# Where the TensorE operands of an attention and mixture-of-experts kernel begin in the on-chip memory

## The reference

```python
# layer 1, on layernorm(x); 4 heads of 128
Q, K, V = xh @ Wh, kh @ Wh, vh @ Wh            # the same Wh for all three
masked = (Q @ K.T / sqrt(128)) * decay_mask
A = maximum(abs(masked.sum(batch)), 1.0)       # summed over the 4 batches
O = A @ V;  Y = normalize(O) * gamma + beta
x = x + (relu(xn @ wg_w) * Y) @ wo_w
# layer 2, on layernorm(x): mixture of experts, 2048 tokens
scores = softmax(xt @ Wg.T)                    # 16 experts in 4 groups
# the 2 best groups, then the 4 best experts of them for each token
h = silu(xt @ W1[e].T) * (xt @ W3[e].T)        # 512 -> 352
y = sum over the 4 experts of weight * (h @ W2[e].T)
z = silu(xt @ Ws1.T) * (xt @ Ws3.T) @ Ws2.T    # shared, 2 x 352 wide
x = x + y + z
```

## The kernel before

| tensor | role on TensorE | before | after | rest before | rest after |
|---|---|---|---|---|---|
| `whi`, `wlo` | moving, experts | 88800, 123616 | 88832, 123648 | 32, 32 | 0, 0 |
| `xhi`, `xlo`, p = 0 | stationary, up | 166624, 170720 | 166656, 170816 | 32, 32 | 0, 0 |
| `xhi`, `xlo`, p = 1 | stationary, up | 168672, 172768 | 168736, 172896 | 32, 32 | 32, 32 |
| `hhi`, `hlo` | stationary, down, even | 178528, 180064 | 178688, 180224 | 32, 32 | 0, 0 |
| `hhi_odd`, `hlo_odd` | stationary, down, odd | 202144, 203680 | 202336, 203872 | 32, 32 | 32, 32 |
| `wg_hi`, `wg_lo` | moving, gate | 88800, 96992 | 88832, 97024 | 32, 32 | 0, 0 |
| `xn_hi`, `xn_lo` | stationary, gate | 158432, 162528 | 158464, 162560 | 32, 32 | 0, 0 |
| `q_hi`, `q_lo` | moving, scores | 52960, 61152 | 52992, 61184 | 32, 32 | 0, 0 |
| `ctx_hi`, `ctx_lo` | stationary, scores | 207776, 215968 | 207808, 216000 | 32, 32 | 0, 0 |
| `wo_hi`, `wo_lo` | moving, projection | 141568, 149760 | 141632, 149824 | 0, 0 | 0, 0 |
| `xT`, `xT_lo` | stationary, projection | 215968, 220064 | 216000, 220096 | 32, 32 | 0, 0 |

## Time and profile before

### The profile page before, as it was taken

How to read it: one execution, slowest core, us unless ns; L and a number is a source line. 1 busy time by engine, 2 the same in 40 slices (tenths; PEclk the granted TensorE clock), 3 DMA queues, 4 the chain that set the end, 5 groups by cost and what they waited for, 6 DMA issues and landing times.

```text
span 919.3 us, 19365 instructions
## 1 busy us (share of the span) xinstructions
PE 899.9 (98%) x4962; PEld 806.1 (88%) x4963; DVE 557.9 (61%) x1105; ACT 332.0 (36%) x708; POOL 494.3 (54%) x346
## 2 busy tenths in 40 slices
PE   8999998899989999999999999999999999999998
PEld 5777887687889999999999999999999999989997
DVE  6656767888896644544444444444444444459997
ACT  4556554354324322333333333333333333332221
POOL 1127777874167764434646664456666643136772
PEclk9999999999999999999999999999999999999999
DMA  6829996665569956878778776788777755588984
GB/s 214 264 106 385 388 403 251 230 189 172 184 227 297 308 206 207 243 205 247 245 235 252 248 246 203 237 244 258 248 251 249 248 170 158 163 231 241 275 254 144
DMA packets 180649, 218.97 MB, mean 238 GB/s; under 512 B 56576, under 2 KB 124160, under 8 KB 180224
## 3 DMA queue, kind: packets, MB, share of 16 engines
q1 hardware_dynamic: 118080, 123.49, 41.9%
q0 software_dynamic: 20816, 79.44, 26.1%
q10 hardware_dynamic: 41712, 15.54, 6.3%
HBM read 127.38 MB, written 91.03 MB: 238 GB/s over the span
## 4 chain that ended last, share of the span: by engine, by line
PE 80%; DVE 9%; issue 4%; ACT 3%; DMA 3%; ACTq 0%; DVEq 0%; POOL 0%; SPq 0%; POOLq 0%
PE ps L1170 15%; PE ps L1171 15%; PE ps L1172 15%; PE ps L1222 8%; PE ps L1224 8%; PE ps L1223 8%; PE ps L1019 2%; PE ps L1035 2%; PE ps L966 1%; DVE st L1469 1%; DVE res L1467 1%; PE ps L1055 1%; PE ps L1057 1%; PE ps L1056 1%; DVE st L1284 1%
## 5 line engine op out<-in xcount | busy, mean ns | idle before, releaser
L1170 PE MATMUL ps<-whi,xhi 128*128 (+1 forms) x888 | 288.8, 325 | 1.2 <-issue 0.6
L1172 PE MATMUL ps<-whi,xlo 128*128 (+1 forms) x888 | 286.7, 323 | 0.0
L1171 PE MATMUL ps<-wlo,xhi 128*128 (+1 forms) x888 | 286.7, 323 | 0.0
L1544 DVE TENSOR_TENSOR hrow<-ps,sg 128x352 f32<-128x352 f32 x95 | 49.7, 523 | 214.1 <-ACT sg L838 214.1
L1170 PEld LDWEIGHTS ps<-whi,xhi 128*128 128x128 f32 x888 | 167.7, 189 | 6.1 <-issue 1.3
L1171 PEld LDWEIGHTS ps<-wlo,xhi 128*128 128x128 f32 x888 | 167.7, 189 | 3.9
L1172 PEld LDWEIGHTS ps<-whi,xlo 128*128 128x128 f32 x888 | 167.3, 188 | 0.0
L838 ACT ACTIVATE sg<-ps 128x352 f32<-128x352 f32 x111 | 51.5, 464 | 268.1 <-PE ps L1172 268.0
L845 ACT ACTIVATE xhi<-ps 128x512 fp32r<-128x512 f32 x112 | 66.9, 597 | 145.8 <-DVE ps L1505 145.7
L566 POOL TENSOR_TENSOR wlo<-raw,whi 128x2816 fp32r<-128x2816 f32 x16 | 100.7, 6291 | 2.4 <-POOL whi L564 0.9
L658 POOL DMA_INDIRECT raw<-yslot_d,sloti x64 | 67.7, 1058 | 57.7 <-DMA yslot_d<-ysb 22.6
(11 more groups left out here) (201 smaller groups left out, 1583.4 us busy)
## 6 DMA issues: line engine op xcount, KB each, us to landing
raw<-wexp_in POOLq DMA_DIRECT2D x18, 2176.0 KB, 11.1
xslot_d<-zero SPq DMA_DIRECT2D x10, 2048.0 KB, 21.6
xg<-xslot_d SPq DMA_DIRECT2D x320, 64.0 KB, 2.8
yslot_d<-ysb SPq DMA_DIRECT2D x80, 256.0 KB, 2.4
h_d<-hrow ACTq DMA_DIRECT2D x79, 192.0 KB, 3.0
hblk<-h_d SPq DMA_DIRECT2D x79, 192.0 KB, 2.5
xg<-xn_d SPq DMA_DIRECT2D x128, 64.0 KB, 3.7
xq<-x_in SPq DMA_DIRECT2D x16, 256.0 KB, 3.3
```

The source lines that it names most:

```text
L1170: pe.matmul(ps[:, bank, 0:INTER], xh, wh, start=(k == 0), stop=False)
L1171: pe.matmul(ps[:, bank, 0:INTER], xh, wl, start=False, stop=False)
L1172: mm = pe.matmul(ps[:, bank, 0:INTER], xl, wh, start=False, stop=(k == KT - 1))
```

## The change

Three pads are added (`line_pad`, `odd_pad`, `row_pad`, each 32 bytes in a partition), `heads_keep` grows by 48 bytes, and each half of `xhi` and `xlo` grows by 32 bytes, so that the second half starts 32 bytes past a multiple of 64; the two instructions that write whole halves take the first 512 columns. No instruction is added, removed or moved on any engine: without the line numbers the lists of instructions of the two programs are the same. What differs is addresses, those of the table above and of all tensors named behind `line_pad`: input tiles, sums and buffers of the other engines too. Line numbers behind the pads grow by 1 to 3.

```diff
         cbf = keep("cbf", [P, 2, P], BF16)
+        keep("line_pad", [P, Q // 4], F32)
         res = keep("res", [P, NT * D], F32)
...
-            late.enter_context(nc.sbuf_tensor("heads_keep", [P, KT * D + B * S + 2 * HCOL + AT_COL + HD + H * S + B + 2 * D], F32))
+            late.enter_context(nc.sbuf_tensor("heads_keep", [P, KT * D + B * S + 2 * HCOL + AT_COL + HD + H * S + B + 2 * D + 12], F32))
...
-        xhi = sb3("xhi", [P, 2, KT * P], F32R)
-        xlo = sb3("xlo", [P, 2, KT * P], F32R)
+        xhi = sb3("xhi", [P, 2, KT * P + Q // 4], F32R)
+        xlo = sb3("xlo", [P, 2, KT * P + Q // 4], F32R)
...
         scat = sb3("scat", [P, XR, D], F32)
+        sb3("odd_pad", [P, Q // 4], F32)
         hhi.append(sb3("hhi_odd", [P, IC * P], F32R))
         hlo.append(sb3("hlo_odd", [P, IC * P], F32R))
+        sb3("row_pad", [P, Q // 4], F32)
         hrow = sb3("hrow", [P, 2, IC * P], F32)
...
-                    act.activation(xhi[:, p, :], ps[:, p, :], ACT.Copy).then_inc(x_hi, 1)
+                    act.activation(xhi[:, p, 0:KT * P], ps[:, p, :], ACT.Copy).then_inc(x_hi, 1)
...
-                    dve.tensor_tensor(xlo[:, p, :], ps[:, p, :], xhi[:, p, :].bitcast(F32), ALU.subtract).then_inc(x_lo, 1)
+                    dve.tensor_tensor(xlo[:, p, 0:KT * P], ps[:, p, :], xhi[:, p, 0:KT * P].bitcast(F32), ALU.subtract).then_inc(x_lo, 1)
```

## The result

The kernel after takes 924.94 us (median of 20 runs), the kernel before 921.25 us (20 runs). The ratio is 1.003, with a 95% interval from 1.0019 to 1.0041: slower by about 0.3%, 1.8 to 3.8 us. The forecast was 921.5 us, no change, with a range of 907 to 929 us. So the time lies in the range, which is wide, and just about at the bound of 0.3% that the prediction drew between "the same" and "slower"; the interval excludes no change at all.

A forecast was written before the change was run, and what follows sets the result against it. TensorE's matmul pace was taken to bound the kernel's expert tiles. Terms 2.0 + 1.3 - 2.2 - 0.7 = +0.4 us on the 919.3 us span gave 919.7; with 1.8 for the median, 921.5 us, range 907 to 929.

The forecast's parts named there:

- the order of the two down sets: Expert tiles, sign in the timeline: even down set goes to 2.06 us and odd one to 2.10, reversing their order.
- That only TensorE's pace counts: Expert tiles: only the matmuls' own pace counts; the other engines were given 0, in the front part too.
- Odd down, +2.0 us from the projection's row: Odd expert tiles, down sets: operands half a line apart cost 4.1 ns a matmul, as in the projection, +2.0 us.
- Odd up, +1.3 us from 1 ns each: Odd expert tiles, up sets: 1 ns a matmul, taken between 0 and 4.1 ns, +1.3 us.
- Even down, -2.2 us: Even expert tiles, down sets: leaving their slow place gains 4.4 ns a matmul, -2.2 us, other end 0.
- three of four places: At 512 columns, places with operands in the same or a near place said to give 229 to 230 ns.
- Even up, 0: Even expert tiles, up sets: no change, staying at 3.83 us a set.
- Moving operands at the start of a line, 0 between -27 us and a little above: Even tiles and front part: one 64-byte line fewer a matmul could save 6.7 ns, -27 us in all; taken as 0.
- both faster rivals: Same place on a line start is good, 913 us (chance 0.26); rest 32 causes the excess, 894 or 858 us (0.08).
- Projection, -0.7 us: Front part, projection: operands coming to the same rest gain 4 ns a matmul, -0.7 us, between 0 and that.
- The slower rival: Odd expert tiles: half-line offset costs 4.1 ns on all 33 matmuls, +7.4 us, 928.5 us; chance 0.22.
- The rule of two read ports: TensorE: with independent SBUF read ports relative places would not count, only moving-stream terms remain, and the time is 921.1 us.

The follow-up runs named there:

- e4: TensorE-only program with the sets in the kernel's order, 39 blocks at chosen addresses; a round takes 11.82 us at before's addresses, 11.89 us at after's.
- e6: The kernel before with only the odd down operands (hhi_odd, hlo_odd) 32 bytes further: 927.32 us, ratio 1.006.
- e1: TensorE-only program giving the first table of pitches, repeated sets of one kind at chosen addresses: down sets 227.1 to 234.5 ns a matmul, by distance.
- e2: The kernel after without its odd offset, so every tensor starts on a multiple of 64 bytes: 919.74 us, ratio to before 0.9986.
- e3: The kernel before with the pads of xhi, xlo, hhi_odd and hrow but not line_pad, weights staying at rest 32: 925.55 us, ratio 1.0039.
- block 0 against 5: TensorE alone: before's addresses, against the same with only the odd down operands moved by 32 bytes: rounds of 11.82 and 11.92 us.
- e9: The kernel before with all four odd stationary buffers 32 bytes further and every other distance kept: 926.94 us, ratio 1.0058.
- block 9: TensorE alone at before's addresses, with odd up and odd down operands both moved by 32 bytes: rounds of 11.96 and 11.90 us.

## Why the prediction was right, and where it was not

The time was in the range, but the range of 22 us holds most outcomes, and the point was "no change" where there is a small one. Of the signs that were named, the order of the two down sets did turn round (231.2 even, 233.1 odd), the odd sets took the 2.10 and, with 3.87, nearly the 3.86 us that were forecast, and the gate stayed. But the pair did not stay within 0.05 us of 11.82: it took 11.893. The even down set was to fall from 2.09 to 2.06 us and fell to 2.08, the even up set rose from 3.83 to 3.85, and the projection did not come down to the gate.

*That only TensorE's pace counts.* Right: the whole difference is in pitches, and e4 shows it again with nothing else running.

*Odd down, +2.0 us from the projection's row.* 4.1 ns a matmul were forecast from the earlier trace rows, 4.3 measured. But the reason does not hold, so the size was luck. The projection lost only 1 to 2 ns when its operands came to the same rest, so most of its slowness was not its half line; by the first table a distance of 160 is slow, and its new one of 128 nearly as slow.

*Odd up, +1.3 us from 1 ns each.* 1.2 ns measured. The 1 ns was a choice between 0 and 4.1, and e6 shows that what an up set takes is also decided by the down set in front of it, of which the prediction knew nothing: luck again.

*Even down, -2.2 us.* This term failed: -9 ns a set instead of -40, -0.5 us. It took for granted that a same rest is a good place. The gap of 4.4 ns between even and odd was itself too large: nine pitches in steps of 0.01 us read to 1 ns only, and the finer starts give 232.2 - 228.8 = 3.4. The "three of four places" are two of three in the rows, the odd down set and the gate. The new distance, 0, is good only in a row of its own kind (226.9 ns in e1) and not between up sets as they stand in the kernel (231.2).

*Even up, 0.* Mis-sized: +15 ns a set, +0.8 us. I had looked at the rest on division by 64 and overlooked that the wider halves of `xhi` push `xlo` from distance 0 to 64. Block 8 of e4 moves nothing but `xlo` by 64 bytes, in both parities: 11.88 us a pair, with 160.5 ns in the even up set instead of 159.6.

*Moving operands at the start of a line, 0 between -27 us and a little above.* The value was right, and e2 measures it in the routed tiles: nothing. With it both faster rivals fall. (The 4119 matmuls of that term rightly count all expert tiles, though its first sentence names the even ones: both kinds stream the same weights.)

*Projection, -0.7 us.* 1 to 2 ns a matmul instead of 4, so -0.2 to -0.3 us.

The sum with what was measured is 39 + 28 - 9 + 15 = 73 ns x 55 pairs = 4.0 us, less the 0.2 to 0.3 of the projection, in place of 0.4; from the first up matmul to the last the traces show the same +4.0 us. The forecast's point was 3.4 us low: 1.7 since the gain of the even down sets hardly came, 0.8 for the even up sets, about 0.4 each for the projection and for the odd tiles. The slower rival, a half line costing 4.1 ns on all 33 matmuls of an odd tile (928.5 us), had the right sign and place but about twice the size: 67 ns an odd tile instead of 135.

*The rule of two read ports.* The Trainium skill (TensorE: Matmul & The Clock Gate, section Step-by-step: what each phase is for) says that loading the stationary operand does not steal bandwidth from the running matmul. The prediction put a time of 921.1 us beside it. Here the traces do not agree in full: with TensorE alone at work, moving nothing but the stationary operands changes a down matmul from 228 to 233 ns (e1) and a pair from 11.80 to 12.00 us (e4). Whether the two reads share anything, or something else of the places counts, the runs do not tell.

What stays open is the mechanism inside: why the pattern repeats after 256 bytes, why a set's pace reaches into the next, and why some places have two paces by turns. That the change acts through relative places is shown (e2, e3, e4); what in the chip makes them count is not.

## What to carry to other kernels

In a stretch that TensorE's pace bounds, the distance modulo 256 bytes between a moving operand and the stationary one loaded beside it was worth up to 1.7% of a pair of tiles here (11.80 to 12.00 us), and a common shift of all operands by 32 bytes nothing; a pad in front of one buffer changes this for every buffer behind it. The effects do not add, so test the whole sequence of sets in a small program of TensorE alone before laying out a kernel by a table of single pitches; here it gave the routed pair of all eight kernels that it repeated to 0.01 us, even where two times alternate. And read a pitch over many tiles: those of the gate range from 228.7 to 232.7 ns at one and the same distance.

## What the runs showed of the hardware that was not expected

- A matmul's pitch depends on the place of the stationary operand relative to the moving one, with a pattern that repeats after 256 bytes: 227 to 234 ns at 512 columns of float32r, 159 to 161 at 352 in sets of one kind, at a granted clock of 1.00 (e1).
- A common shift of 32 bytes changes no set of the routed tiles by more than 1 ns (e2 against before, e3 against after).
- The same up sets take 160.0 or 163.0 ns a matmul, depending on the address of the down set in front of them alone (e4, block 0 against 5; before against e6).
- The same pair at the same distances can take 11.906 and 11.961 us by turns (e9), with TensorE alone too (e4, block 9).
- In the routed tiles starts of matmuls repeat to 1 or 2 ns from pair to pair while DMAs, VectorE, ScalarE and GpSimd are busy beside them: no trace of their traffic is in TensorE's pace there. In the gate, tiles at the same distances range from 228.7 to 232.7 ns.
